# Stage one of a two-layer graph kernel: the dense rows are left out of the steps of the table fill and taken in later steps

## The reference, cut to what matters

```python
h = relu(layernorm(x))
gate = silu(edge_attr @ W1.T + b1) @ W2.T + b2
gate += sum(emb[z[src]] * (emb[z[dst]] @ adaptW.T), -1, keepdims=True)
msg = gate * h[dst] * (cutoff(distance) * mult[dst])[:, None]
agg = segment_sum(msg, src) / clip(segment_sum(mult[dst], src), 1e-8)[:, None]
x = x + layernorm(h + agg) * gamma + beta
```

## Time and profile before

| | us |
|---|---|
| runs, median (lowest to highest of 3) | 1542.93 (1542.01 to 1545.06) |
| the profiled execution's own time | 1533.91 |
| its span | 1532.2 |
| VectorE busy | 1336.7 (87%) |
| TensorE busy | 1157.1 (76%) |
| POOL busy | 1025.5 (67%) |
| ScalarE busy | 618.2 (40%) |
| mean granted TensorE clock | 0.598 |

### The profile page before, as it was taken

The page is one execution under the profiler, slowest core; times in us unless marked ns, Lnnn a source line. Parts: engine busy times, 40 slices in busy tenths (PEclk is TensorE's granted clock), DMA queues, the critical chain, the costliest instruction groups (busy, mean ns, idle before and its releaser), DMA issues.

```text
span 1532.2 us, 20105 instructions
## 1 busy us (share of the span) xinstructions
PE 1157.1 (76%) x5198; PEld 846.7 (55%) x5198; DVE 1336.7 (87%) x3937; ACT 618.2 (40%) x1423; POOL 1025.5 (67%) x809
## 2 busy tenths in 40 slices
PE   5898999989999989991047878888888888886000
PEld 2677777777777777771035555555555555554000
DVE  6999999999999999880299999999999999993598
ACT  2544444544445444440034444444444444442000
POOL 7655567777887676666537887887878878866100
PEclk9756555655556565555556565555655655557555
DMA  7999986666666566642446665555555555533899
GB/s 228 305 320 333 325 228 155 153 145 145 142 164 154 136 155 138 147 103 11 130 156 169 170 161 139 140 139 140 138 137 139 140 141 139 140 71 58 295 396 390
DMA packets 154389, 268.72 MB, mean 175 GB/s; under 512 B 73818, under 2 KB 90411, under 8 KB 153380
## 3 DMA queue, kind: packets, MB, share of 16 engines
q1 hardware_dynamic: 78228, 223.53, 43.5%
q0 software_dynamic: 68992, 24.64, 17.5%
q10 hardware_dynamic: 7056, 19.27, 3.1%
HBM read 194.33 MB, written 112.55 MB: 200 GB/s over the span
## 4 chain that ended last, share of the span: by engine, by line
PE 32%; DMA 20%; DVE 19%; POOL 15%; issue 11%; ACT 3%; SPq 1%; POOLq 0%; ACTq 0%; DVEq 0%
POOL agg L468 11%; PE ps_m L555 11%; DMA t<-agg,src_all 6%; PE ps_m L644 6%; PE ps_qs L555 4%; DMA agg<-x,once 3%; PE ps_k L630 3%; DMA lows<-low 2%; DVE x L1038 2%; DVE same L834 2%; DMA agg<-y,once 2%; DVE t L1042 2%; POOL nodes L426 2%; DMA agg<-ysq,once 2%; POOL agg L504 2%
## 5 line engine op out<-in xcount | busy, mean ns | idle before, releaser
L504 POOL DMA_INDIRECT agg<-sums,once x196 | 317.8, 1621 | 89.5 <-issue 64.1
L426 POOL DMA_INDIRECT nodes<-in_table,dst_all x196 | 194.1, 990 | 104.0 <-issue 50.2
L495 POOL DMA_INDIRECT t<-agg,src_all x196 | 190.3, 971 | 83.7 <-issue 49.1
L555 PEld LDWEIGHTS ps_m<-msg,same 128*128 128x128 f32 x980 | 200.4, 314 | 29.8 <-issue 29.8
L555 PE MATMUL ps_m<-msg,same 128*128 128x48 f32 x980 | 208.2, 398 | 1.0 <-issue 1.0
L630 PE MATMUL ps_k<-h_t,rw_sb 56*128 56x256 f32 x588 | 132.3, 571 | 96.3 <-ACT hid L724 73.7
L555 PEld LDWEIGHTS ps_qs<-msg,same 128*128 128x128 f32 x980 | 183.0, 288 | 2.1 <-DVE msg L926 2.1
L555 PE MATMUL ps_qs<-msg,same 128*128 128x49 f32 x980 | 180.1, 362 | 2.0 <-DVE msg L926 2.0
L468 POOL DMA_INDIRECT agg<-x,once x84 | 135.1, 1609 | 49.0 <-issue 21.9
L630 PEld LDWEIGHTS ps_k<-h_t,rw_sb 56*128 56x128 f32 x588 | 67.6, 260 | 144.6 <-ACT hid L724 100.6
L644 PE MATMUL ps_m<-hid,rw_sb 128*64 128x256 f32 x588 | 136.1, 634 | 0.0
(11 more groups left out here) (149 smaller groups left out, 2575.1 us busy)
## 6 DMA issues: line engine op xcount, KB each, us to landing
agg<-in_both SPq DMA_DIRECT2D x14, 2758.0 KB
t<-agg SPq DMA_DIRECT2D x49, 784.0 KB, 4.4
kept<-kept_out SPq DMA_DIRECT2D x49, 404.0 KB, 2.8
kept_in<-kept SPq DMA_DIRECT2D x49, 404.0 KB
agg<-bias_rows SPq DMA_DIRECT2D x49, 384.0 KB
out<-t ACTq DMA_DIRECT2D x49, 384.0 KB, 5.8
rows<-in_src_rows SPq DMA_DIRECT2D x49, 256.0 KB, 4.1
rows<-in_dst_rows SPq DMA_DIRECT2D x49, 256.0 KB, 3.2
```

The source lines that it names most:

```text
L426: pool.indirect_dma_start(nodes[s][:, t, :], None, table, bass.IndirectOffsetOnAxis(ap=dst_all[:, c:c + 1], axis=0)).then_inc(nodes_in[b % ...
L495: pool.indirect_dma_start(t2[b % T2S][:, t, :], None, wide, bass.IndirectOffsetOnAxis(ap=src_all[:, c:c + 1], axis=0)).then_inc(ends_in[b ...
L504: pool.indirect_dma_start(agg1, bass.IndirectOffsetOnAxis(ap=once1[b % LAG1][:, t:t + 1], axis=0), sums1[b % LAG1][:, t, :], None, compute ...
L555: last = mm(ps[:, t * width:(t + 1) * width], kept_same[:, at:at + P], m[:, v, :], start=(v == t), stop=(v == TILES - 1))
```

## The change

Stage one's chunks are no longer tied to its blocks. `chunks_of(b)` gives no chunk for the 14 steps of the fill, and one or two for each of the 35 steps behind: 1, 1, 2, 1, 2 and so on, 49 in all. The first chunk of a step (`mid`) stands on VectorE at the old place, a second one (`late`) between logit and msg.

- TensorE: the first chunk's `centred(c + 1)` now stands between the transposes and `sums0(b - 1)`, a second one's behind `h1(b + 1)`. `ps_c` has two buffers, and so has `dc`.
- ScalarE: the square root is split in two, one for the block (`estd0`), one for the chunk (`dense_std`). `hidden(c + 1)` runs for each chunk of the step, behind `gate_hidden(b + 1)`.
- SP: chunks are loaded and stored by c. Five constants (gamma, beta, rb2, norm, rel) are loaded in step 1 (`late_in`), the second layer's weights in step 14. `bias_rows` is made in step 2.
- POOL: the second gather of a pre-run step waits for `logit_done` instead of `pc_done`.

```diff
-CONSTS = 13
+CONSTS = 8
+LATE = 5
+DRY = FILLS
+def chunks_of(b):
+    if b < DRY:
+        return []
+    left = NBLOCK - DRY
+    return list(range((b - DRY) * NBLOCK // left, (b + 1 - DRY) * NBLOCK // left))
...
@@ SP @@
+                if b == DRY - 2:
+                    load_xt(0)
+                    load_xt(1)
                 if b + 2 < NBLOCK:
                     load_lows(b + 2)
-                    load_xt(b + 2)
                     load_rows(b + 2)
                     load_feat(b + 2)
+                for c in chunks_of(b):
+                    if c + 2 < NBLOCK:
+                        load_xt(c + 2)
+                if b == 1:
+                    load_late()
+                if b == FILLS:
+                    load_weights()
...
-                sp.wait_ge(S["std_done"], b + 1)
-                sp.wait_ge(S["pc_done"], b + 1)
-                sp.dma_start(kept[b], kept_out[b % 2][:, :]).then_inc(kept_stored[b % 2], 16)
+                for c in chunks_of(b - 1)[1:] + chunks_of(b)[:1]:
+                    store_kept(c)
@@ POOL @@
-                pool.wait_ge(S["pc_done"], step + 1)
+                pool.wait_ge(S["logit_done"], step + 1)
@@ TensorE, centred(c) @@
-                need(pe, S["rl_done"], c)
-                need(pe, S["sqd_done"], c)
+                need(pe, S["rl_done"], c - 1)
+                need(pe, S["sqd_done"], c - 1)
@@ TensorE, step b @@
                 last.then_inc(S["turned_t_done"], 1)
+                for c in chunks_of(b)[:1]:
+                    if c + 1 < NBLOCK:
+                        centred(c + 1)
                 if b > 0:
                     sums0(b - 1)
...
                 if b + 1 < NBLOCK:
                     h1(b + 1)
-                    centred(b + 1)
+                if b == DRY - 1:
+                    centred(0)
+                for c in chunks_of(b)[1:]:
+                    if c + 1 < NBLOCK:
+                        centred(c + 1)
@@ ScalarE, step b @@
+                for c in chunks_of(b - 1)[1:] + chunks_of(b)[:1]:
+                    dense_std(c)
                 act.wait_ge(S["var_e_done"], b + 1)
-                act.wait_ge(S["var_d_done"], b + 1)
-                need(act, kept_stored[b % 2], 16 * (b // 2))
-                A(kept_out[b % 2][:, PC:PC + G], kept_out[b % 2][:, PC + G:KEPT], ACT.Sqrt, ...)
+                need(act, S["rstd_done"], b)
+                A(estd0[:, :], evar0[:, :], ACT.Sqrt, ...)
                 if b + 1 < NBLOCK:
                     gate_hidden(b + 1)
-                    hidden(b + 1)
+                if b == DRY - 1:
+                    hidden(0)
+                for c in chunks_of(b):
+                    if c + 1 < NBLOCK:
+                        hidden(c + 1)
@@ VectorE, step b, behind logit, coef_r and type_of(b + 1, 2 and 3) @@
+                if b == DRY - 1:
+                    dense_sum(0)
+                    dense_centre(0)
+                if b == 2:
+                    dve.wait_ge(S["late_in"], 16 * LATE)
+                    V.tensor_copy(bias_rows[:, :, :], each(rb2_b[:, :], NR)).then_inc(S["vec_set"], 1)
+                for c in late:
+                    if c + 1 < NBLOCK:
+                        dense_sum(c + 1)
+                    dense_var(c)
                 dve.wait_ge(S["logit_done"], b + 1)
                 dve.wait_ge(S["gate_done"], b + 1)
                 V.tensor_tensor(glog[:, :, :], ...)
+                for c in late:
+                    if c + 1 < NBLOCK:
+                        dense_centre(c + 1)
+                    dense_mean(c)
                 V.scalar_tensor_tensor(out=hdst[:, :, :], ...)
                 V.tensor_tensor(raw[:, :, :], ...)
+                for c in late:
+                    dense_out(c)
```

More of the change, by code:

```diff
@@ L63 @@
 POOL_SET = 15
-CONSTS = 13
+CONSTS = 8
[6 more added lines that the diff above has]
+    return list(range((b - DRY) * NBLOCK // left, (b + 1 - DRY) * NBLOCK // left))
+assert sum((chunks_of(b) for b in range(NBLOCK)), []) == list(range(NBLOCK))
+assert max(len(chunks_of(b)) for b in range(NBLOCK)) == 2 and len(chunks_of(DRY)) == 1
 def place(t):
@@ L569, in _ @@
                 lookup(0, t)
-            centred(0)
             for b in range(NBLOCK):
@@ L677, in _ @@
             gate_hidden(0)
-            hidden(0)
             for b in range(NBLOCK):
@@ L803, in _ @@
             V.tensor_tensor(cw_a[:, :], cw_all[:, :], cw_b[:, :], ALU.max).then_inc(S["vec_set"], 1)
+            for s in range(2):
+                V.memset(kept_out[s][:, PC:KEPT], 0.0).then_inc(S["kept_set"], 1)
             def low_masks(b):
@@ L892, in _ @@
                     type_of(b + 1, 1)
-                    dense_centre(b + 1)
-                dve.wait_ge(S["rsum_done"], b + 1)
-                V.scalar_tensor_tensor(out=kept_out[s][:, 0:PC].rearrange("p (r f) -> p r f", r=NR), in0=cols(rsum[:, :], H),
-                                       scalar=-1.0 / H, in1=rl[s][:, :, :], op0=ALU.mult, op1=ALU.add).then_inc(S["pc_done"], 1)
+                for c in mid:
+                    dense_out(c)
                 dve.wait_ge(S["std_done"], b + 1)
-                V.reciprocal(rstd[:, :], kept_out[s][:, PC:PC + TILES]).then_inc(S["rstd_done"], 1)
+                V.reciprocal(rstd[:, :], estd0[:, :]).then_inc(S["rstd_done"], 1)
                 dve.wait_ge(S["q_done"], b + 1)
```

115 lines of the change are left out of this document (73 added, 42 removed).

## The result

| | before | changed |
|---|---|---|
| runs, median (lowest to highest), us | 1543.99 (1542.01 to 1546.87), 4 | 1621.68 (1618.32 to 1629.78), 4 |
| ratio, 95% interval | | 1.0522 (1.0472 to 1.0572) |
| the profiled execution's own time, its span | 1533.91, 1532.2 | 1623.51, 1621.8 |
| VectorE, TensorE, POOL, ScalarE busy | 1336.7, 1157.1, 1025.5, 618.2 | 1333.9, 1166.8, 1023.4, 622.5 |
| mean granted clock | 0.598 | 0.608 |

Slower by 78, where 57 was forecast (1600, range 1555 to 1660). Every engine is as busy as before within 10; the 90 between the two spans is waiting.

What follows compares the result with a forecast made beforehand. POOL's adds bound stage one (744); after the change, steps paced by a TensorE-VectorE ring: 212 + 1 + 574 - 2 + 15.6 = 801, +57. Profiled 1533.9 + 57 = 1591, plus 9.0 to the median: 1600 us, range 1555 to 1660.

Steps and rivals of the forecast that it cites:

- T(0) = 21.0: Start of low_hot on VectorE in step 0, forecast at 21.0 us instead of 23.63.
- Fill steps 13.65, T(14) = 212: Steps 0 to 13, without dense work, take 13.65 us each, so step 14 starts at 212, with 213.5 before.
- Adds from 214: POOL's stage-one adds start at 214 us, no earlier than before; with 529 of work they end at 743.
- Single steps 14.3: The 21 late steps with one chunk: 13.2 us fast, 15.96 slow with centred in the ring, mean 14.3.
- Double steps 19.6: The 14 late steps with two chunks: 17.5 us fast, 22.8 slow, mean 19.6.
- The share of fast steps: Part of the late steps where TensorE's clock rises: taken as 0.6, with 14 of 34 before.
- The wait of `dense_var`: In double steps VectorE's dense_var waits for ScalarE's sqd, behind h1: 3 to 6 us, 50 or more over 14 steps.
- Tail 15.6: Work behind the steps for stage one's last block: sums, copy, four adds and landing, 15.6 us.
- A: Rival, chance 0.13: no stall in double steps, ScalarE has sqd ready; double steps 17.0, +21 us, 1564.
- C: Rival, chance 0.09: fill steps run at VectorE's pace, 11.5 us, POOL still the bound; -30 us, 1513.
- D: Rival, chance 0.03: TensorE at full clock everywhere, fill steps 9.2 us; -45 us, 1498.
- B: Rival, chance 0.12: TensorE's clock hardly rises; +146 us, 1689 at a share of 0, about +110 at 0.2.

Runs made afterwards that it cites:

- experiment 4: The kernel before with only the late loads: five constants in step 1, second layer's weights in step 14, bias_rows in step 2; 1528.20 us, ratio 1.0007.
- Kernel 1: The changed kernel with fill chunk b issued only once the logits of block b - 1 are done; 1594.48 us on chip P, ratio 1.0452.
- kernels 6 and 7: First: hidden early with centred between transposes and sums only in double steps, 1578.27 us. Second: also only 5 steps without chunks, fill in 12 steps, 1559.48 us.
- hidden early: The changed kernel with ScalarE's hidden of the first chunk ahead of gate_hidden in double steps; 1558.45 us on P, 1590.16 on R.

## Why the prediction was right, and where it was not

The direction, the mechanism of the double steps and the range held; the fill steps were missed on all chips but P, and that the late steps came out within 10 is in part luck. By the terms of the sum, on the profiled execution:

- *T(0) = 21.0*: 21.2. Right. Nor did the late loads cost anything (experiment 4).
- *Fill steps 13.65, T(14) = 212*: wrong, T(14) came at 237.9, and this is the step of the working that failed. The changed kernel took 23.5 in step 0 (+9.9) and 14.86 in the 13 others (+1.21 each, 15.7). What the prediction had right is that they don't fall with the dense work gone: VectorE lost a third of its busy time there, and the steps got no shorter. On chip P the three kernels without dense rows in the fill have step 0 at 10.2 to 10.9 and the others at 13.66 to 13.70, the 13.65 forecast to 0.05. Kernel 1 there, which keeps the double steps as they are, has its first gather at 801.1, where the sum has 801 (T(14) at 208.8 and the late steps 577 to 578, against 212 and 574). On the other chips the step isn't TensorE's ring any more but goes through the copy of the sums to the block's square root. The prediction had no such term: it let everything behind `sums0` follow its modelled end, as in the earlier trace rows.
- *Adds from 214*: 239.3, which is T(14) + 1.4, against the + 2 that the forecast had. POOL's second gather waits for the logits 55.2 in 11 steps where it had 32.5 in 13 for pc_done, and, as forecast, nothing hangs on it.
- *Single steps 14.3*: 14.43; by themselves 12.8 to 13.5 where the sums ran at full and 15.6 to 15.8 where all ran at half, against 13.2 and 15.96, and 15.0 to 15.6 where the clock rose only after the sums.
- *Double steps 19.6*: 20.36; 17.2 and 22.4, against 17.5 and 22.8, with the same third kind at 20.6. The share of fast steps was the uncertain part: 4 of 13 doubles here, 8 on Q, 6 on R, and 9 of 21 singles here, where 0.6 was taken. The late steps together took 583 against 574, and this is luck: with the measured shares the forecast's own prices would have given 607. The third kind, which the prediction didn't have, took back some 14 (9 singles at 0.7, 3 doubles at 2.2); the rest is in steps a little cheaper than forecast and in the last one.
- *The wait of `dense_var`*, forecast as 3 to 6 and 50 or more in all: 3.81 at half, 2.0 to 2.1 in the third kind, 0.6 to 0.9 in fast steps, 31.6 in 13. The 50 didn't follow from the working: with its share of 0.6, 3.9 in slow steps and 1 to 1.7 in fast ones make 30 to 36.
- *Tail 15.6*: 14.8, 836.2 - 821.4.
- *POOL is no bound any more*: right for the changed kernel. The 743 that I gave POOL's chain would not have held, though: where the steps ended earlier (kernels 6 and 7), it took 557 and 559 in place of 529.
- *+9.0 from the profiled execution to the median*: wrong, and it hid a third of the miss. Stage one ended 35 over the 801 and stage two was 3 shorter, so the profiled 1623.5 is 32.5 over the forecast 1591. The median lies 1.8 under the profiled execution instead of 9.0 over it, and so only 21.7 over 1600. The profile of before has a step 0 of 12.8, and its relatives on Q and R have 20.2 and 20.9. That its median there is 9 to 10 above the one on P fits with this, but no trace of the kernel before itself was taken on those chips, so this is argued, not shown.

The rivals: A (no wait in the double steps) is what hidden early built, and it is worth 31 in the trace on R, and 15 by the ratios, where the working gave 36. C (faster, since the fill steps go at VectorE's pace) fell with the fill steps: on no chip was their mean under 13.6. D: the mean clock from 220 on is 0.60. B's slow steps came in part: in the first trace 6 of 13 doubles ran at half throughout, and 3 more until behind the sums.

Of the rule that was weighed: in hidden early on R, h1 runs at full (1.06 for its two matmuls, 1.94 at half), then TensorE is idle 1.89, and the lookups that follow are at half, 0.53 each:

```profile
296.68 1.06 PE L583 MATMUL ps_m<-feat,w1t_sb 40*48 40x512 f32 x2
...
299.62 0.51 PE L576 MATMUL ps_k<-types_lo,low_hot 128*128 128x392 bf16 x1 [1.89 <-DVE low_hot L867]
299.92 0.53 PE L577 MATMUL ps_k<-types_lo,low_hot 128*128 128x392 bf16 x1
```

The Trainium skill, TensorE: Matmul & The Clock Gate, section "HAM oscillation — how this bites in real kernels", lets only longer idle gaps do this; the traces of after disagree with it as the one of before did.

## What to carry to other kernels

Work that lies in the shadow of another engine's ring costs nothing where it is: taking it out there gave 0 (on P, fill steps of 13.7 with it and without), and putting two portions into later steps cost some 30 in the traces, 15 by the ratios, through one wait (24.7 in 13 steps, 1.9 each) and what stands behind it, and 0.7 to 0.9 a step through centred in the ring. Before moving work, ask of each instruction behind which queue entry its input is made; reordering two entries on ScalarE gave back 15 of the 66 that the change cost on R by the ratios, and some 30 in the traces. When the start of a bound chain is what matters, look at what its first instruction waits for: issuing the same fill in half chunks over 12 steps instead of 14, with a shorter pre-run, was worth 0.8%, moving the work was not.

## What the runs showed of the hardware that was not expected

- The same kernel (hidden early) took 210.3 to its step 14 on one chip and 237.4 on another, in one session each: 12 of it in step 0, the rest in fill steps of 14.8 instead of 13.7. The kernel before differs by 9 to 10 in its median between those chips. A change's ratio can hold such a part; two chips with one kernel show it.
- In most of these fill steps of the changed kernel and its variants, on three of four chips or sessions, a semaphore behind the sums is seen 1.7 to 1.8 after the modelled end of the last matmul, some 3 where the sums are short, and 0.04 after it from step 14 on, when the fill is over. The cause is open.
- A chain of adds on POOL took 525 to 534 in four kernels and 557 and 559 in two others from the same instructions, with longer waits for the adds to land; the cause is open.
